# TensorE's step as one run of 60 large products and one block of small ones, transposes in two row halves, all queues in a new order

## What is computed

```python
def reference(x, itok_B_0_15, itok_B_3_7, ...):          # x: 128 x 32 x 512
    x = x + attn(cond(x, itok_B_0_15, W), w_qkv, ln..., w_out)
    x = x + ffn(cond2(x, W2, itok_B_3_7), gate_w, up_w, down_w, fc1_w, fc2_w, expert_w, ln...)
    return x
# cond : einsum('bct,bcd->bdt', x, W[condition])          one 32 x 32 "style" matrix per sequence
# attn : q, k, v = split(clip(h @ w_qkv.T, -8, 8)); q, k = layer_norm(q), layer_norm(k)
#        32 heads of 16, causal scores with ALiBi bias, softmax, probs @ v, then @ w_out.T
# cond2: einsum('bsi,boi->bso', x, W2[adapter])            one 512 x 512 "adapter" matrix per sequence
# ffn  : shared = relu(y @ up_w)**2 @ down_w
#        routed = ((y @ fc1_w) @ expert_w * sum(top2(y @ gate_w))) @ fc2_w
#        return layer_norm(shared + routed)
```

## Time and profile before

| what | value |
|---|---|
| time, median of 3 runs | 1127.82 us (1126.93 to 1128.59) |
| the profiled execution's own time | 1126.27 us |
| its span, first to last instruction | 1124.5 us |
| PE / PEld busy | 1088.2 us (97%) / 890.1 us (79%) |
| POOL busy | 713.4 us (63%) |
| DVE busy | 676.1 us (60%) |
| ACT busy | 602.5 us (54%) |
| mean granted TensorE clock | 0.994 of full speed |

### The profile page before, as it was taken

The page is one execution under the profiler, slowest core; times in us unless marked ns, Lnnn a source line. Parts: engine busy times, 40 slices in busy tenths (PEclk is TensorE's granted clock), DMA queues, the critical chain, the costliest instruction groups (busy, mean ns, idle before and its releaser), DMA issues.

```text
span 1124.5 us, 27403 instructions
## 1 busy us (share of the span) xinstructions
PE 1088.2 (97%) x10996; PEld 890.1 (79%) x10996; DVE 676.1 (60%) x1040; ACT 602.5 (54%) x985; POOL 713.4 (63%) x612
## 2 busy tenths in 40 slices
PE   5999999999999999999999999999999999999994
PEld 3878788888888888888877778787878888787883
DVE  5567666666666667667666245565655565554432
ACT  4466767676767677777776425335161625333220
POOL 4566888788888887878676464556455464533342
PEclk9999999999999999999999999999999999999997
DMA  7125555646464646565567953233514123030101
GB/s 277 41 79 182 171 201 166 202 160 212 158 209 158 214 152 219 172 211 156 201 226 234 375 166 95 85 96 106 113 48 133 59 90 99 29 85 29 47 29 37
DMA packets 95292, 160.77 MB, mean 143 GB/s; under 512 B 46400, under 2 KB 47168, under 8 KB 89792
## 3 DMA queue, kind: packets, MB, share of 16 engines
q1 hardware_dynamic: 79456, 118.16, 32.6%
q0 software_dynamic: 12224, 34.10, 9.5%
q10 hardware_dynamic: 3488, 6.78, 1.7%
HBM read 93.97 MB, written 42.47 MB: 121 GB/s over the span
## 4 chain that ended last, share of the span: by engine, by line
PE 95%; DMA 1%; issue 1%; DVE 1%; POOL 0%; ACT 0%; SPq 0%; DVEq 0%; ACTq 0%; POOLq 0%
PE bank L648 24%; PE pair L832 15%; PE bank L808 15%; PE bank L738 10%; PE bank L688 8%; PE bank L825 8%; PE pair L665 3%; PE bank L696 3%; PE pair L710 3%; PE bank L638 3%; PE bank L723 1%; PE bank L778 1%; PE bank L676 1%; DMA xt<-in_x,tile_rows 1%; PE bank L759 0%
## 5 line engine op out<-in xcount | busy, mean ns | idle before, releaser
L1675 POOL TENSOR_TENSOR w_lo<-w2t,w_hi 128x2048 fp32r<-128x2048 f32 x38 | 174.8, 4600 | 39.6 <-ACT w_hi L994 36.2
L648 PE MATMUL bank<-wqkv_hi,h_hi 128*128 128x512 f32 x384 | 153.9, 401 | 0.2
L648 PE MATMUL bank<-wqkv_hi,h_lo 128*128 128x512 f32 x384 | 150.0, 391 | 0.0
L648 PE MATMUL bank<-wqkv_lo,h_hi 128*128 128x512 f32 x384 | 149.7, 390 | 0.0
L1745 POOL TENSOR_TENSOR u_lo<-act,u_hi 128x512 fp32r<-128x512 f32 x64 | 82.7, 1292 | 103.3 <-ACT u_hi L1187 103.2
L808 PE MATMUL bank<-yT_hi,up_hi 128*128 128x512 f32 x256 | 100.8, 394 | 0.0
L808 PE MATMUL bank<-yT_hi,up_lo 128*128 128x512 f32 x256 | 99.8, 390 | 0.0
L1524 DVE TENSOR_TENSOR act<-act 128x512 f32<-128x512 f32 x59 | 67.0, 1135 | 54.6 <-ACT act L1183 54.6
L808 PE MATMUL bank<-yT_lo,up_hi 128*128 128x512 f32 x256 | 99.6, 389 | 0.0
L832 PE MATMUL pair<-down_hi,u_hi 128*128 128x512 f32 x256 | 99.6, 389 | 0.0
L832 PE MATMUL pair<-down_lo,u_hi 128*128 128x512 f32 x256 | 99.6, 389 | 0.0
(11 more groups left out here) (178 smaller groups left out, 2908.8 us busy)
## 6 DMA issues: line engine op xcount, KB each, us to landing
w2t<-in_w SPq DMA_DIRECT2D x38, 1024.0 KB
vx<-v_hl SPq DMA_DIRECT2D x128, 68.0 KB
x1g<-x_rows SPq DMA_DIRECT2D x32, 256.0 KB, 3.0
kx<-k_hl SPq DMA_DIRECT2D x124, 64.0 KB
x_rows<-x1t SPq DMA_DIRECT2D x31, 256.0 KB
ffn_high<-w_high SPq DMA_DIRECT2D x20, 256.0 KB, 3.6
ffn_low<-w_low SPq DMA_DIRECT2D x20, 256.0 KB, 3.3
stage<-in_wqkv SPq DMA_DIRECT2D x3, 1024.0 KB, 9.4
```

Source lines behind the costliest of these rows:

```text
L648: m = e.matmul(into, a[:, c, :], b[:, n, c, :], start=(c == 0 and k == 0), stop=(c == KC - 1 and k == 2))
L1675: e.tensor_tensor(w2_lo[:, :, :], w2t[:, :, :], w2_hi[:, :, :].bitcast(F32), ALU.subtract).then_inc(d_wlo, 1)
```

## The change

TensorE's step becomes q, k, v, adapter, output projection (60 large products in one run), then values, style of the next tile, turn_slot of the **next** slot, turn_q, turn_k, turn_values, scores. The slot's, q's and k's transposes, and the values' for tiles 0 to 27, are made as two of 64 rows and 64 moving columns each instead of one of 128 x 128; their results lie as two halves in a pair of banks (`banks45`, `banks67`). Scaling and splitting of q and k are one step later than before (tile i - 2 in step i), the softmax chain too (tile i - 3); `high_w2`, `low_w2` and `turn_slot` are one step earlier (slot i - 5 in step i). The tail is written anew, and several waits follow the new banks.

The core of the diff (the loops of the five queues, and what is new in the functions):

```diff
+    def half(banks, n):
+        return banks[:, :, n * KC * HALF:(n + 1) * KC * HALF].rearrange("p g (c t) -> p g c t", c=KC)
...
             for c in range(KC):
-                    m = e.transpose(into[:, P * c:P * c + P], src[:, P * c:P * c + P], ident)
+                    for g in range(ROW_TILES):
+                        rows = slice(HALF * g, HALF * g + HALF)
+                        m = e.transpose(into[:, g, c, :], src[rows, P * c:P * c + P], ident[rows, rows])
...
# SyncE
-            for i in range(T - 1):
-                if i >= 4:
-                    spread_v(i - 3)
-                if i >= 5:
-                    store_x1(i - 5)
...
-                if i >= 5:
-                    load_w2(i - 5)
...
-                if i >= 1:
-                    spread_k(i - 1)
+            for i in range(T):
...
+                if i >= 5:
+                    store_x1(i - 5)
+                if i >= 3:
+                    spread_v(i - 3)
...
+                if 0 <= i - 6 < CHUNKS:
+                    keep_chunk(i - 6)
+                if 0 <= i - 5 < CHUNKS:
+                    load_chunk(i - 5)
...
+                if i >= 2:
+                    spread_k(i - 2)
+                if LAG - 1 <= i < T - 1:
+                    load_w2(i - LAG + 1)
+                if T - 9 <= i < T - 1:
+                    load_planes(i - T + 9)
...
# TensorE
+            for i in range(T):
+                if i in (1, 2):
                     style(i + 1)
                 project_q(i)
...
+                if i == 2:
+                    make_route(2)
+                    make_route(3)
                 project_k(i)
                 project_v(i)
...
                 if i >= LAG:
                     adapt_slot(i - LAG, B2)
                 if i >= 4:
                     out_project(i - 4)
...
                 if i >= 3:
                     values(i - 3)
...
+                if SHORT - 1 <= i < T - 1:
+                    style(i + 1)
+                if LAG - 1 <= i < T - 1:
+                    turn_slot(i - LAG + 1, half(banks45, 0))
+                if i >= 1 and i != 3:
+                    turn_q(i - 1)
+                    turn_k(i - 1)
...
+                if i >= 3:
+                    turn_values(i - 3)
+                if i >= 2:
+                    scores(i - 2)
...
# ScalarE
-                if i >= LAG:
-                    high_w2(i - LAG)
-                if i >= 1:
-                    normalize(i - 1)
...
+                if i >= SHORT:
+                    high_h(i)
...
+                if i >= 2:
+                    scale_q(i - 2)
+                    scale_k(i - 2)
+                    high_q(i - 2)
+                    high_k(i - 2, k_hl)
...
+                if i >= 3:
+                    soft_exp(i - 3)
...
+                if LAG - 1 <= i < T - 1:
+                    high_w2(i - LAG + 1)
...
# VectorE
+                if i >= SHORT:
+                    low_h(i)
+                if i >= 3:
+                    bias_max(i - 3)
...
                 if i >= 3:
                     turn_probs(i - 3)
...
+                if i >= 2:
+                    low_q(i - 2)
+                    low_k(i - 2, k_hl)
...
+                if i >= 3:
+                    divide(i - 3)
...
# GpSimd
-                upto(e, "o", i - 4)
...
+                if i >= 3:
+                    subtract_max(i - 3)
...
-                if i >= LAG:
-                    low_w2(i - LAG)
...
+                if LAG - 1 <= i < T - 1:
+                    low_w2(i - LAG + 1)
```

More of the change, by code:

```diff
@@ L67 @@
 EARLY_GROUPS = 2
+ROW_TILES, HALF = 2, P // 2
 CLIP = 8.0
@@ L408, in slot_at, with by_half, h_bank, q_banks @@
         return (1, 3) if m else (5, 6)
-    def k_bank(t):
-        return B4 if t < 3 else B5
+    def half(banks, n):
+        return banks[:, :, n * KC * HALF:(n + 1) * KC * HALF].rearrange("p g (c t) -> p g c t", c=KC)
+    def by_half(tile):
+        return tile.rearrange("p c (g t) -> p g c t", g=ROW_TILES)
+    def h_bank(t):
+        return B6 if t < 2 else B5 if t < SHORT else B2
+    def q_banks(t):
+        return half(banks67 if t < T - 1 else banks45, 0)
+    def k_banks(t):
+        return half(banks67 if t < T - 1 else banks45, 1)
+    turned_values = banks45[:, :, KC * HALF:2 * KC * HALF]
+    def value_bank(t):
+        return B3 if t == T - 4 else B6
+    def slot_halves(tile):
+        return by_half(tile.rearrange("p (c t) -> p c t", c=KC))
+    def out_bank(t):
+        return B3 if t <= T - 4 else B7
     def route_bank(c):
-        return pair[:, 0, :] if c == 0 else B7
+        return pair[:, c % 2, :]
     def last_slot(m):
@@ L719, in turn_slot @@
                     e.wait_ge(s_routec, KC)
-                elif s <= LAST:
-                    e.wait_ge(d_tl, s)
-                for c in range(KC):
-                    m = e.transpose(into[:, P * c:P * c + P], xg[s % 2][:, P * c:P * c + P], ident)
+                if s <= LAST:
+                    upto(e, "cv", s + LAG - 1)
+                    upto(e, "olo", s + LAG - 5)
+                    e.wait_ge(r_low, min(s + 1, CHUNKS))
+                    if s:
+                        e.wait_ge(d_tl, s)
+                for c in range(KC):
+                    if s <= LAST:
+                        for g in range(ROW_TILES):
+                            rows = slice(HALF * g, HALF * g + HALF)
+                            m = e.transpose(into[:, g, c, :], xg[s % 2][rows, P * c:P * c + P], ident[rows, rows])
+                    else:
+                        m = e.transpose(into[:, P * c:P * c + P], xg[s % 2][:, P * c:P * c + P], ident)
                 m.then_inc(d_t, 1)
```

486 lines of the change are left out of this document (234 added, 252 removed).

## The result

| | before | after |
|---|---|---|
| time, median of 4 runs | 1127.7 us (1126.9 to 1128.6) | 1193.7 us (1192.1 to 1195.3) |
| ratio, 95% interval | | 1.0585 [1.0566, 1.0603] |
| the profiled execution's own time, and its span | 1126.27, 1124.5 us | 1195.31, 1193.5 us |
| q of tile 6 starts at | 102.86 us | 117.92 us |
| 25 steps, q of tile 6 to q of tile 31 | 471.6 us, 18.86 each | 512.8 us, 20.51 each |

The change costs 66 us, 5.9%; the forecast was 1179 us, from 1150 to 1203. Of the 69.0 us by which the span grew, 15.1 lie before q of tile 6, 41.2 in the 25 steps, 8.3 in the attention tail and 4.5 behind it.

What follows compares the result with a forecast made beforehand. The prediction took TensorE's own work (18.83 us per step) as the bound before, and a 20.6 us ring through four queues after. 1126.3 + 43.4 + 7.5 + 1 = 1178.2, made 1179 us; range 1150 to 1203.

Steps and rivals of the forecast that it cites:

- The ring: Middle steps: circle of waits through four queues and a DMA, once per step, 20.6 us; 25 steps cost +43.4 us.
- Each alone is hidden.: Moves of high_w2, low_w2, low_q/low_k and load_w2 between or within queues: any one by itself stays covered.
- TensorE's work: TensorE's own work in a middle step after the change: 18.4 us, between 17.6 and 20.2.
- the transposes: TensorE's small products in each step: halves cost the same as wholes, between 0.87 us gained and 1.75 us lost.
- one change-over less: TensorE's step: one entry from small into large products instead of two, a gain of 0.3 to 0.4 us.
- Each step ends with TensorE idle for about 2.2 us before q: End of each of 25 middle steps: TensorE waits for h_lo about 2 us, near 50 us in total.
- The front: Before q of tile 6: later scores of tile 0 and a longer step 5, +7.5 us, between 5 and 10.
- The tail: From q of tile 31 to up(0, 5): 52 us of products plus 4 to 5 of waits, +1 us.
- The three terms: Parts of the forecast's added time: middle steps +43.4 us, before q of tile 6 +7.5, attention's end +1.
- Rival 1: Middle steps: the ring is open, TensorE stays the bound, faster; 1105 to 1120 us, say 1115; chance 0.08.
- The rule I set beside it: Whole kernel: the skill's advice to relieve the busiest engine first, cited in support of Rival 1.
- Rival 3: Middle steps: longer ring, or TensorE slow as well with a lower clock; 22 us per step, 1213 us; chance 0.05.

Runs made afterwards that it cites:

- The best of those that open the ring and leave no product out: Changed kernel with the load of the adapter weights ahead of spread_k again on SyncE's queue; 1157.7 us, ratio 1.0265.
- the one with two links out: Changed kernel with high_h ahead of high_w2 on ScalarE and low_q/low_k ahead of turn_probs on VectorE; 1160.9 us, ratio 1.0295.
- the shifted kernel: The one with two links out, with 60 small products more ahead of the loop of steps; a single execution took 1169.6 us.

## Why the prediction was right, point by point, and where it was not

**The ring.** Right in place, links and size: 20.6 us forecast, 20.51 measured, 41.2 us more for the 25 steps where the sum had 43.4. Load to copy was 4.97 us (5.05), the load's issue 0.77 us after kx (0.8), and each link within 0.1 us of its row. The Trainium skill's estimate ("DMA: Bandwidth & Descriptors", Anatomy of one DMA; 4.4 us for the load) would have given 19.9.

**"Each alone is hidden."** Wrong, and no step of the sum depended on it, so the time did not show it. The load behind kx costs 34 us by itself. The rows for it were there: 5.1 us of cover against a shift of 5.6.

**TensorE's work.** 18.4 us forecast, 18.2 measured where nothing stalls. For the transposes I took no change against a range from -0.87 to +1.75 us; for those of q and k alone in the kernel before, the net is zero, and with the whole block it is -0.37 us. For one change-over less I took 0.3 to 0.4 us; the run of large products is 0.23 us shorter (13.85 against 8.40 + 2.96 + 2.72). The Trainium skill's rule ("TensorE: Matmul & The Clock Gate", Part 3, The mechanism), that weight loads overlap when they go to another row group, fits the 16 halves themselves (0.67 us for 0.87, and 0.51 in the changed kernel, where they stand among other halves). Part of that gain is paid again where halves and whole rows meet, and TensorE's work did not come down to 17.6 us.

**"Each step ends with TensorE idle for about 2.2 us before q", near 50 us in total.** Wrong in kind: 16.8 us in 16 waits for `h_lo`, and 31 us in waits without a name, most of them the 21 instruction stalls (28.0 us from product to product), which I had not thought of. Under the ring they cost little, since a stalled TensorE only eats the wait for `h_lo`; the time came out right because the ring is the longer of the two. That I had missed a second limit did no harm here by luck: with the ring open the stalls are the limit, and without the ring the forecast would have been too low.

**The front, +7.5 us between 5 and 10.** It was +15.1 at q of tile 6, outside its range. 8.2 us were there at q of tile 5, where I had 4: the late kx of tile 0 held scores until 61.14, as placed, and behind that wait the clock fell: q of tile 3 took 7.38 us for 24 products instead of 5.69, in a window (62.55 to 77.18) with a granted clock of 0.87, so partly at the lower of the two levels, 1.2 GHz. And step 5 took 22.9 us, not 19.7, because the first load took 7.65 us from issue to copy. The chain and the two rows of that load:

```profile
61.14 1.48 PE pair L760 x88
62.62 7.38 PE bank L677 x24
...
107.05 0.36 SPq L482 DMA_DIRECT2D w2t<-in_w  x1
...
114.70 1.91 ACT L1057 ACTIVATE w_hi<-w2t 128x2048 fp32r<-128x2048 f32 x1 [8.64 <-DMA w2t<-in_w]
```

**The tail, +1 us between -3 and +5.** It was +12.8. I counted its products (52 us) and put 4 to 5 us on waits; the chain has 5.52 us for kx of the last tile alone, a nameless stall of 2.25 us, and behind up(0, 5) a wait of 5.49 us for the split of a slot whose load went out at 707.89, because on SyncE's queue it stood behind a wait of 14.0 us for the stores of x1 to land:

```profile
663.68 5.52 DMA kx<-k_last
...
710.59 5.49 issue
```

The three terms were 43.4, 7.5 and 1; they measured 41.2, 15.1 and 12.8. The 17 us between the sum (1178.2) and the profiled execution (1195.3) are -2.2 + 7.6 + 11.8: all of the excess lies in the two terms that I sized roughly, and both came out above their ranges. The total stayed within 1150 to 1203 because that range was wider than the errors of the terms.

**The rivals.** Rival 1 (the ring is open, 1115 us) did not happen, but its price was wrong too: with the ring opened by two moves the kernel takes 1160.9 us and not 1115. The rule I set beside it (the Trainium skill, "Perfetto Trace Analysis", Identifying the Most-Contended Engine) would have led to the same mistake: TensorE has less work per step in the changed kernel (18.2 us for 18.8), and this kernel and all that were made from it are slower than before. Rival 3's clock effect was there, small: 0.97 in the 25 steps, and q of tile 3 as above.

**A better kernel?** None of these beats the kernel before. The best of those that open the ring and leave no product out, 1157.7 us, is 2.7% above it. With neither ring nor stalls 18.2 us per step are in reach by the chains, 25 x 0.66 = 16.5 us under before; the longer front and tail and what is behind it cost 28 us in the changed kernel, and still 21 in the one with two links out (8.3 before q of tile 6, 8.3 in the tail, 4.2 behind it). I leave open what of these can be had.

## What to carry to other kernels

Before work is moved between queues, walk once round every circle that a step closes, DMAs and issue times included, and compare it with the step; one line moved on SyncE's queue cost 34 us here, because it used up a cover of 5.1 us that no row of idle time shows. A better order of the busiest engine is worth nothing if it makes the step wait for a chain that used to fit beside it. And gathering all small instructions in one block lets TensorE use them up faster than they come: here a piece of 16 KB, some 123 products with their weight loads, took some 3.6 us to arrive and 3.0 to use up. Look for waits without a name at a fixed distance in the stream; large products between groups shorter than a piece, as in the kernel before, went without them. A large load that passes just then may make the wait longer.

## What the runs showed of the hardware that I had not expected

- TensorE pauses for its own instructions: 15 to 25 stalls in each kernel with the whole block, of 0.6 to 5.5 us from product to product. They stand at 191 or 192 modulo 256 when all its records are counted, in 123 of the 128 stalls of the first table, and at 191 to 193 in the shifted kernel. The trace puts them down as "issue".
- What goes with them is a piece of 256 records used up in under 4 us: none in the kernel before, 19 to 25 in the others with the whole block, of which 14 to 21 end in a stall in the five of the second table.
- Those packets seldom start while a 1 MB load passes: in three kernels 1 of 178 started 1.2 to 3.8 us after the load's issue, and 62 in the 2.2 us behind that. They also follow TensorE's own progress, so this is not the load's doing alone.
- Half-row transposes are cheap among themselves: 16 in 0.51 us against 8 whole ones in 0.87. Alone between whole-row work they take 0.67 us, and the products behind them 0.20 us more.
- TensorE's granted clock was lower in the kernels in which it waited more: 0.957 of full speed (2.4 GHz is 1, 1.2 GHz 0.5) with a wait of 2.4 us in the mean in most steps, 0.972 with the ring, 0.994 before.
- The same 1 MB load took 4.97 us from issue to copy in the middle of the kernel, 6.1 us where k's layout and v's went beside it, and 7.65 us when the first one met the early traffic.
